# Normalising rows and adding x on GpSimd in the attention stage of a fused transformer block

## What is computed

```
x = x + _layernorm(_L0_attn_ref(_layernorm(x), ...))
xf = _layernorm(x)                      # input of the ffn
probs = softmax((norm(xf) * ln_scale + ln_bias) @ gate_w.T)      # top 2 of 8 experts
out = swiglu(xf, shared) + sum over experts of w[:, e] * swiglu(xf, expert e)
x = x + _layernorm(out)
```

## Time and profile before

| | us |
|---|---|
| median of 3 runs (lowest to highest) | 849.85 (846.43 to 853.27) |
| profiled execution | 846.51 |
| its span in the profile | 844.8 |
| PE busy | 694.6 (82%) |
| DVE busy | 603.4 (71%) |
| ACT busy | 504.1 (60%) |
| POOL busy | 323.1 (38%) |
| exponentials on ACT, L1463, x640 | 325.3, mean 557 ns |
| row maxima on DVE, L342, x288 | 340.6, mean 1219 ns |
| POOL's masks, L1380, x128 | 83.8, mean 667 ns |

### The profile page before, as it was taken

The page is one execution under the profiler, slowest core; times in us unless marked ns, Lnnn a source line. Parts: engine busy times, 40 slices in busy tenths (PEclk is TensorE's granted clock), DMA queues, the critical chain, the costliest instruction groups (busy, mean ns, idle before and its releaser), DMA issues.

```text
span 844.8 us, 17266 instructions
## 1 busy us (share of the span) xinstructions
PE 694.6 (82%) x6111; PEld 336.6 (40%) x6142; DVE 603.4 (71%) x1252; ACT 504.1 (60%) x1055; POOL 323.1 (38%) x437
## 2 busy tenths in 40 slices
PE   5887289999998898978888979879788856798886
PEld 2332023333343233323333324323277745677662
DVE  6899578888879888758888857886255552355465
ACT  3664056778777796666787656867655422244454
POOL 3775112212212321535231443433542244455574
PEclk9998589999999999989999989997999988899998
DMA  5456260121212213212123121007031121154264
GB/s 149 140 158 177 78 174 16 34 47 49 46 31 46 69 33 71 62 48 62 31 55 87 33 77 49 30 15 231 29 78 60 42 73 44 45 141 112 75 195 143
DMA packets 88784, 66.18 MB, mean 78 GB/s; under 512 B 27727, under 2 KB 75248, under 8 KB 88702
## 3 DMA queue, kind: packets, MB, share of 16 engines
q1 hardware_dynamic: 80076, 54.24, 24.8%
q0 software_dynamic: 4352, 8.99, 3.2%
q10 hardware_dynamic: 4274, 1.87, 0.9%
HBM read 38.11 MB, written 24.46 MB: 74 GB/s over the span
## 4 chain that ended last, share of the span: by engine, by line
PE 44%; DVE 20%; ACT 8%; issue 6%; another core or an unknown queue 4%; DMA 3%; SPq 2%; POOL 2%; ACTq 0%; DVEq 0%; POOLq 0%
DVE block_max L342 11%; PE ps L2017 10%; PE ps L2044 8%; PE ps L327 5%; PE ps L2124 4%; ACT expT L1463 4%; PE ps L334 2%; PE ps L1994 2%; SPq L1204 2%; PE ps L2113 2%; DMA q_space<-negT 2%; PE ps L2105 1%; PE ps L2082 1%; PE ps L2107 1%
## 5 line engine op out<-in xcount | busy, mean ns | idle before, releaser
L1463 ACT ACTIVATE expT<-ps 128x512 f32<-128x512 f32 (+1 forms) x640 | 325.3, 557 | 151.6 <-PE ps L2044 140.8
L342 DVE TENSOR_REDUCE block_max<-ps 128x8 f32<-128x1024 f32 x288 | 340.6, 1219 | 65.6 <-PE ps L327 44.6
L2017 PE MATMUL ps<-expT,vr 128*9 128x256 f32 (+1 forms) x2560 | 183.3, 368 | 16.2 <-ACT x_in L1423 12.6
L2044 PE MATMUL ps<-q_space,k_space 64*128 64x512 bf16 (+3 forms) x768 | 170.1, 340 | 15.7 <-DMA q_space<-negT 6.7
L327 PE MATMUL ps<-k_space,q_space 64*128 64x128 bf16 (+3 forms) x1152 | 135.3, 284 | 40.4 <-DVE block_max L342 24.2
L1380 POOL TENSOR_SCALAR_AFFINE_SELECT expT<-expT 128x512 f32<-128x512 f32 x128 | 83.8, 667 | 198.5 <-ACT expT L1463 198.4
L2044 PEld LDWEIGHTS ps<-q_space,k_space 64*128 64x128 bf16 x768 | 46.9, 94 | 163.7 <-ACT expT L1463 102.4
L1395 POOL DMA_INDIRECT expert_rows<-expT,tile_to x72 | 70.6, 980 | 91.3 <-ACT expT L1498 66.9
L327 PEld LDWEIGHTS ps<-k_space,q_space 64*128 64x128 bf16 x1152 | 50.8, 96 | 79.4 <-DVE block_max L342 55.9
L2017 PEld LDWEIGHTS ps<-expT,vr 128*9 128x9 f32 x2560 | 42.3, 89 | 98.9 <-issue 47.2
L1333 POOL TENSOR_SCALAR negs<-block_max 128x32 bf16<-128x32 f32 x16 | 4.7, 294 | 146.8 <-DVE block_max L1583 146.8
(11 more groups left out here) (244 smaller groups left out, 953.0 us busy)
## 6 DMA issues: line engine op xcount, KB each, us to landing
expT<-sorted_rows SPq DMA_DIRECT2D x72, 65.0 KB
q_parts<-parts SPq DMA_DIRECT2D x24, 128.0 KB, 2.3
k_parts<-parts SPq DMA_DIRECT2D x24, 128.0 KB, 2.3
q_space<-q_parts SPq DMA_DIRECT2D x32, 96.0 KB
k_space<-k_parts SPq DMA_DIRECT2D x32, 96.0 KB
expT<-expert_rows SPq DMA_DIRECT2D x10, 256.0 KB, 4.2
v_ones<-v_st SPq DMA_DIRECT2D x8, 288.0 KB, 3.1
vr<-v_ones SPq DMA_DIRECT2D x16, 144.0 KB
```

The source lines that it names most:

```text
L342: nc.vector.reduce_max(bm[:, g % 2, 2 * f:2 * f + 2, at:at + 4], ps[:, 2 * odd:2 * odd + 2].rearrange("p h (n k) -> p h n k", k=P), AX_X). ...
L1463: act.activation(expT[:, (NS * g + s) % PTN, hh, 0:width], ps[:, B_S + n % S_RING, 0:width], ACT.Exp, scale=SCALE).then_inc(exp_ok, 1)
L2017: last = nc.tensor.matmul(ps[32 * hh:32 * hh + VW, B_O, at:at + n], vr[:, g % RING, kt, hh * VW:(hh + 1) * VW], expT[:, (NS * g + s) % PTN ...
L2044: last = nc.tensor.matmul(ps[:, B_S + n % S_RING, col:col + m], head_rows(kr, g, hh, slice(kt * P, (kt + 1) * P)), head_rows(qr, g, hh, sl ...
```

## The change

Three things, all for batches 0, 1 and 2. The 48 normalising instructions on ACT (24 of projected rows, 24 of rows with x) are gone; a new function `scale_rows` makes each of them as one POOL instruction (multiply by the row's inverse root, add the shift, both read per partition), four in step 6 and four in step 7 of the groups with r = 1 and with r = 2. The six adds of x leave DVE's slots 0 and 2 and become POOL instructions in steps 0 and 1 of the groups with r = 2, behind the masks of these steps. The last batch stays as it was.

```diff
+        def scale_rows(pool, k, c, src, out):
+            pool.wait_ge(shifted[k], c + 1)
+            if k == 1:
+                wait(pool, sent, scattered(c // 2))
+            for t in range(NT):
+                last = nc.gpsimd.tensor_scalar(out[:, t], src[:, t], rstd[:, k, c, t:t + 1], nb[:, k, c, t:t + 1], ALU.mult, ALU.add)
+            last.then_inc(normed[k], 1)
...
+                    if q >= 0 and r == 2 and s in (0, 1):
+                        c = 2 * q + s
+                        pool.wait_ge(normed[0], c + 1)
+                        pool.wait_ge(at_in[c % 2], DMA * AT_DMAS * (c // 2 + 1))
+                        nc.gpsimd.tensor_tensor(x_rows[:, c % 2], x_rows[:, c % 2], at_rows(c), ALU.add).then_inc(mid_ok, 1)
                     if q >= 0 and r == 2 and s == 4:
                         root(pool, 1, 2 * q)
                         root(pool, 1, 2 * q + 1)
+                    if q >= 0 and r == 1 and s in (6, 7):
+                        c = 2 * q + s - 6
+                        scale_rows(pool, 0, c, at_rows(c), at_rows(c))
+                    if q >= 0 and r == 2 and s in (6, 7):
+                        c = 2 * q + s - 6
+                        scale_rows(pool, 1, c, x_rows[:, c % 2], xs(q)[:, c % 2, 0, :, 0:E])
...
-                    for i in range(2):
-                        c, t = 2 * q + i, slot - 24 - 6 * i
-                        if r == 1 and 0 <= t < NT:
-                            normalize(act, 0, c, at_rows(c), at_rows(c), [t])
-                        if r == 2 and 0 <= t < NT:
-                            norm_rows(act, c, [t])
...
-                    if at == (2, 0):
-                        add_mid(dve, 2 * q)
-                    if at == (2, 2):
-                        add_mid(dve, 2 * q + 1)
```

## The result

The changed kernel takes 860.95 us (median of 4 runs, 859.59 to 866.51) against 850.55 us (4 runs, 846.43 to 853.27) for the kernel before: a ratio of 1.0147, with an interval of 1.0105 to 1.019. It is slower by over 1%, where I had forecast 852.7 us and a change that can't be told from none. The profiled execution took 861.14 us.

What follows compares the result with a forecast made beforehand. No engine was taken as full: PE, DVE and ACT bound different stretches in turn. Terms -3.2 + 0.8 - 0.2 + 5.5 = +2.9 us on the profiled execution (846.5 to 849.4), forecast as a median of 852.7 us, range 846 to 862.

Steps and rivals of the forecast that it cites:

- everything moves by 0.28 us and no more: Groups 6, 10, 14: statistics wait for POOL's add and start 0.28 us later, shifting what follows; +0.8 us for three batches.
- POOL is let in once between any two instructions of DVE's weight split: Group 14: POOL's calls alternate with DVE's split, so rows are ready at 579.55 and PE is held, +5.5 us.
- the dear call: Rival, chance 0.19: each POOL normalising call costs 0.8 us instead of 0.45, giving 863.5 us; decides from 0.65 us on.
- Projected rows: Groups 5, 9, 13: slots 28 to 39 shrink to the plain length, -1.06 us per batch, -3.2 us.
- The adds: Groups 6, 10, 14: DVE sheds two 0.68 us adds per batch but its statistics wait for POOL; +0.8 us in all.
- Rows with x, groups 6 and 10: PE's transposes wait for POOL's calls and start at 310.3 instead of 310.39: -0.1 us per batch, -0.2 us.
- Group 14: Third batch's rows with x: POOL's calls wait beside DVE's weight split and hold PE's transposes until 579.55, +5.5 us.
- worse-lock rival: Chance 0.13: in group 14 POOL is let in nowhere before 576.7, rows 7.6 us late, sum +5.0, 854.9 us.

Runs made afterwards that it cites:

- The instruction of no use on DVE: The kernel before with one more DVE instruction of 0.68 us ahead of the first statistics in groups 6, 10 and 14, POOL untouched: ratio 1.0079.
- the two edits that shorten PE's gap: The changed kernel with POOL's adds one step earlier (ratio 0.9998), or with the statistics two and four slots later on DVE (ratio 0.9997).
- this part alone: The kernel before with POOL normalising only the eight rows with x of group 14: ratio 1.0087.
- the late statistics: The changed kernel with DVE's statistics two slots (first chunk) and four slots (second chunk) later: ratio 0.9997.
- the projected rows alone: The kernel before with only the projected rows of groups 5, 9 and 13 normalised on POOL: ratio 0.9962.

## Why the prediction was wrong

The forecast was +2.9 us on the profiled execution; it was +14.5 in span. The 11.6 between them are worked out below, step by step. Two steps failed: that behind a later start of DVE's statistics everything moves by 0.28 us and no more, and that POOL is let in once between any two instructions of DVE's weight split. Neither has a term for the half clock behind PE's longer idle time. The time, 860.95, lies in the range of 846 to 862, but that is luck: the range's end was put there by a rival, the dear call, that did not happen.

*Projected rows: right.* -1.06 per batch forecast, -1.11, -1.07 and -1.05 measured; the new calls cost what was worked out from two rows of other operations, 0.45 us, here and at the rows with x of groups 6 and 10:

```profile
L791 POOL TENSOR_SCALAR q_space<-q_space,rstd,shift 128x128 f32<-128x128 f32 x24 | 10.5, 451 | 0.0
...
L791 POOL TENSOR_SCALAR rows<-x_rows,rstd,shift 128x128 f32<-128x128 f32 x24 | 17.6, 746 | 0.0
...
L1365 POOL TENSOR_TENSOR x_rows<-x_rows,q_space 128x512 f32<-128x512 f32 x6 | 7.6, 1271 | 0.0
```

The second row's 746 is no other price: its 24 calls hold the 8.80 us of group 14. Without the four it is 0.44 us each ((17.6 - 8.8)/20).

*The adds: mechanism right, term mis-sized, its effect on the clock left out.* DVE's wait of about 0.8 us was forecast and is 0.88. The add took 1.27 us, not the 1.16 of the earlier trace rows. But "everything behind moves by 0.28" was the wrong step. PE, which needs the maximum behind the statistics, was already waiting 1.37 us there, and now waits 2.05. Counted from the group's start, the statistics begin 0.35 us later, and the instruction that closes them (var_eps) takes 0.39 instead of 0.17 us, now beside a mask of POOL: so the maximum ends 0.58 us later. At full clock steps 2 to 4 grow by 0.59 us (10.92 against 10.33), twice the 0.28. And in this execution all three gaps were followed by 6.8 us at 1.2 GHz in which PE's rows take 1.04 instead of 0.62 us: 2.54, 2.37 and 2.33 us per batch, 7.2 in all against 0.8 forecast. That is +6.4 of the 11.6. The instruction of no use on DVE reproduces it, and the two edits that shorten PE's gap remove it, so the gap is shown as the cause; why it is followed by half clock in some occasions only is not.

*Rows with x, groups 6 and 10: sign right, too small.* -0.1 forecast, -0.53 measured (steps 7 to 9: 7.96 us before, 7.43 after), -0.9 of the difference. I took POOL's eighth call as PE's release and compared only the start of the transposes; in fact the gain of ACT's steps 7 and 8 comes through, as in group 5, and PE has its own work until the second chunk is nearly there.

*Group 14: mechanism right, 1.2 us short, and the clock behind it left out.* Measured from the group's start the last transpose ends at 587.46 - 549.33 = 38.13 us, before at 575.12 - 546.06 = 29.06: 9.07 later, of which 2.33 come from steps 2 to 4, so 6.7 against the forecast 5.5. The kernel with this part alone gives 6.7 too (35.78 - 29.06). The step that failed is "with one POOL call let in between two DVE instructions". The second call waits for the first cast (1.86 us); the third, issued at 575.8, ends at 579.85, behind the subtraction and behind the next cast: DVE got in a second time before it. So it takes 4.06 us and waits for two DVE instructions, and the fourth waits for the second subtraction. POOL's power, which the forecast had beside that subtraction, begins at 582.29, behind it. From the end of the split to the end of POOL's eighth call it is 4.30 us (581.99 to 586.29) instead of the forecast 2.35; 0.8 of these 1.95 come back because DVE, which hardly waits, is through earlier. In the trace of before DVE's cast had been the one that waited, and I made a rule of that one case. The Trainium skill (SBUF — State Buffer, Who interferes with whom) says that whichever of the two issues first gets the shared ports for its whole instruction, and the other blocks fully. The trace agrees that one waits for the other's whole instruction. On who goes first its recorded starts do not agree: the second call starts at 573.95, ahead of the cast at 574.09, and ends 0.24 us behind that cast's end; and the third, waiting since 575.8, was passed over by a cast that started at 578.40.

Behind this wait come 23.9 us at a granted clock of 0.50; the same stretch of before, 9.0 us ahead of group 15's start to 14.9 behind it, has a mean of 0.79. It costs about 1.1 us at the end of group 14 (10.18 = 2.33 + 6.74 + 1.11) and 1.4 us in group 15 (2.2 where the kernel before takes 28.0 us for that group); that these two are the clock's doing is argued from the rows, not shown by a run of its own. I had named this in the worse-lock rival, without a price. Together: group 14 without its steps 2 to 4 grew by 7.85 instead of 5.5 us, group 15 by 1.43, so +3.8.

*What is left.* Groups 7, 8, 11 and 12 +1.5, the start and the tail together +0.8: not caused by an edit that I can name, and the start varies by more between profiles. 6.4 - 0.9 + 3.8 + 2.3 = 11.6.

*The chances.* Slower by over 1% had 0.23, hung on the price of the call (above 0.65 us, or 0.55 with the worse lock). The way that it took was not among the rivals with a price. In the two repeats, whose profiles have half clock behind none and two of the three gaps, the same kernel is slower by 0.6% and 0.75%: still more than the 0.3% of the forecast, but not over 1%. So the size hangs at least in part on an effect that is there in one execution and not in another, which asks for a wider chance of "slower" than 0.23.

## What to carry to other kernels

Price an idle gap of TensorE by its new length, not by its growth: the rows of before show how long PE waits at the place already, and a wait that grew from 1.4 to 2.05 us cost 0.6 us at full clock and 2.4 where half clock followed. When elementwise work moves to GpSimd to free another engine, place its consumer one step later or the work one step earlier, and keep it away from long two-input or casting VectorE instructions, where a call of 0.45 us can take 4. Of such a change keep the parts that gain: here all but the last batch's rows, with the consumer moved, gave -1.25% where the whole change lost 0.6 to 1.5%.

## What the runs showed of the hardware that I had not expected

- In steps 2 to 4 of groups 6, 10 and 14, a PE gap of 2.0 us was followed by TensorE at 1.2 GHz for 3.4 or 6.8 us in 12 of 18 cases, one of 1.4 us or less never in 30. Another gap, of 1.73 to 1.76 us, stands some 1.5 us ahead of step 7 of group 14 in all 16 profiles, those of the kernel before too: in 11 of them 3.4 us of half clock began within 1.8 us behind it.
- During the transposes' waits in group 14 (2.2 to 2.5 us, then 2.8 to 3.3) began 20.5 to 23.9 us of half clock in six of the seven profiles of kernels that have them. In the seventh, with the late statistics (waits of 3.46 and 3.24 us), it was 6.8 us; the next 10.2 begin 3 us into group 15, where the kernels without these waits have them too.
- A GpSimd call of 0.45 us took 4.06 us: it waited through two VectorE instructions of 2.88 and 1.22 us. With no GpSimd instruction beside them, in the kernel with the projected rows alone, these took 2.83 and 1.22 us.
- GpSimd's DMA_INDIRECT rows of line 771, 0.98 us each on average in the kernel before, took 2.03, 3.69 and 2.74 us beside VectorE's weight split, the last of them beside a two-input subtraction alone.
- GpSimd's add of two f32 arrays of 128x512 took 1.27 us, the subtraction of line 472 in the kernel before 1.16.
